# Two mixture-of-experts stages of a graph network kernel: scatter of node rows replaced by an inverted gather, output biases' products moved behind the expert loop

## The reference, cut to what matters

```python
# first layer: three-layer experts, gates are the softmax of the two best scores
for e in range(8):
    h = gelu(x @ W1[e] + b1[e]);  h = gelu(h @ W2[e] + b2[e])
    out += comb[..., e:e+1] * (h @ W3[e] + b3[e])
# second layer: two-layer experts, gates are the two best of the softmax
for e in range(8):
    h = gelu(flat_x @ w1[e] + b1[e])
    out += (h @ w2[e] + b2[e]) * gates[:, e:e+1]
x = x + out          # x inside the experts is layernorm(x)
```

## Time and profile before

| | us |
|---|---|
| median of 3 runs (2336.26 to 2338.91) | 2336.54 |
| the profiled execution's own time | 2320.56 |
| its span, first to last instruction | 2318.8 |
| PE busy | 2096.3 (90%) |
| DVE busy | 1424.1 (61%) |
| ACT busy | 921.7 (40%) |
| POOL busy | 395.6 (17%) |

### The profile page before, as it was taken

One profiled execution on the slowest core, in us unless ns is written; L12 is line 12 of the kernel. 1 busy time (PEld: TensorE's weight loads), 2 busy tenths in 40 slices (PEclk: granted clock), 3 DMA queues, 4 the chain that ended last, 5 costly groups with the idle time before them and its releaser, 6 DMA issues. The chain is left out here.

```text
span 2318.8 us, 32237 instructions
## 1 busy us (share of the span) xinstructions
PE 2096.3 (90%) x12766; PEld 2018.4 (87%) x12766; DVE 1424.1 (61%) x2283; ACT 921.7 (40%) x1220; POOL 395.6 (17%) x216
## 2 busy tenths in 40 slices
PE   6998999999999999999869949788889968999995
PEld 6898999998999999999849949687889947999994
DVE  7654555565763233333459963358985777888885
ACT  2342255554441111111127723125622225777772
POOL 1674200000302444443010022210000020000001
PEclk9999999999999999999969979899999968999997
DMA  6222233333340111110159851110122047999985
GB/s 222 43 49 64 89 121 132 117 116 143 110 143 21 62 42 51 52 52 11 56 198 353 314 194 62 48 46 28 65 75 76 1 155 277 380 368 372 374 346 212
DMA packets 121791, 326.89 MB, mean 141 GB/s; under 512 B 14376, under 2 KB 83016, under 8 KB 106410
## 3 DMA queue, kind: packets, MB, share of 16 engines
q1 hardware_dynamic: 96906, 265.66, 31.9%
q10 hardware_dynamic: 18976, 43.31, 5.2%
q0 software_dynamic: 5760, 15.86, 2.2%
HBM read 278.22 MB, written 46.49 MB: 140 GB/s over the span
## 5 line engine op out<-in xcount | busy, mean ns | idle before, releaser
L666 PE MATMUL banks<-weight_hi,xt_hi 128*128 128x384 f32 (+2 forms) x2208 | 738.3, 334 | 46.2 <-DVE xt_lo L1442 14.3
L669 PE MATMUL banks<-weight_lo,xt_hi 128*128 128x384 f32 (+2 forms) x2208 | 722.8, 327 | 0.0
L670 PE MATMUL banks<-weight_hi,xt_lo 128*128 128x384 f32 (+2 forms) x2208 | 722.3, 327 | 0.0
L666 PEld LDWEIGHTS banks<-weight_hi,xt_hi 128*128 128x128 f32 x2208 | 422.9, 192 | 58.1 <-issue 29.2
L669 PEld LDWEIGHTS banks<-weight_lo,xt_hi 128*128 128x128 f32 x2208 | 422.9, 192 | 0.4 <-issue 0.2
L670 PEld LDWEIGHTS banks<-weight_hi,xt_lo 128*128 128x128 f32 x2208 | 422.1, 191 | 0.0
L1908 DVE TENSOR_TENSOR weight_lo<-weight_raw,weight_hi 128x2304 fp32r<-128x2304 f32 (+2 forms) x153 | 341.0, 2243 | 52.0 <-ACT weight_hi L1170 50.8
L1170 ACT ACTIVATE weight_hi<-weight_raw 128x2304 fp32r<-128x2304 f32 (+2 forms) x153 | 285.8, 1881 | 88.1 <-PE banks L666 56.5
L868 POOL TENSOR_TENSOR weight_hi<-weight_raw,columns 128x2304 fp32r<-128x2304 f32 x20 | 80.6, 4028 | 690.1 <-DMA weight_raw<-L_gnn_root_in 322.6
L1670 DVE TENSOR_TENSOR held_lo<-banks,held_hi 128x384 fp32r<-128x384 f32 x80 | 44.6, 558 | 213.0 <-ACT held_hi L1096 213.0
L2528 PE MATMUL banks<-held_hi,a_rel 128*128 128x384 f32 (+1 forms) x550 | 171.5, 340 | 2.8 <-ACT a_rel L1111 2.8
(11 more groups left out here) (404 smaller groups left out, 3490.2 us busy)
## 6 DMA issues: line engine op xcount, KB each, us to landing
weight_raw<-L_ffn_w_in SPq DMA_DIRECT2D x102, 1152.0 KB, 7.1
weight_raw<-L_gnn_W_in SPq DMA_DIRECT2D x32, 1152.0 KB, 5.5
weight_raw<-L_ffn_W_in SPq DMA_DIRECT2D x17, 1152.0 KB, 8.4
products<-bias_rows SPq DMA_DIRECT2D x80, 192.0 KB, 1.9
slot_in<-slot_rows ACTq DMA_DIRECT2D x34, 384.0 KB, 5.3
slot_out<-bias_rows ACTq DMA_DIRECT2D x34, 384.0 KB, 6.5
weight_raw<-L_ffn_W_in SPq DMA_DIRECT2D x17, 576.0 KB, 8.0
product_back<-products SPq DMA_DIRECT2D x10, 960.0 KB, 4.7
```

What stands on the lines that cost most here:

```text
L666: ins = pe.matmul(dst, s[0], m[0], start=start, stop=False)
L669: pe.matmul(dst, s[0], m[1], start=False, stop=False)
L670: return pe.matmul(dst, s[1], m[0], start=False, stop=stop)
```

## The change

Routing. Instead of sending rows to their places, the kernel stores `XE` once to DRAM (`node_rows`, with a row 0 of zeros, then the nodes), by five plain DMAs that SP issues behind the first weight loads, and inverts the places on chip. DVE splits each place into slot and row, writes two one-hot arrays (`is_row` 10 x 128 wide, `in_slot` 10 x 18 wide, the latter multiplied by the node's number), and PE sums the ten products of them: bank 3 then holds for each slot and row the number of its node, or 0. DVE copies this to `slot_node`, and POOL gathers slot by slot from `node_rows` straight into `slot_in`, two slots at once and then one whenever PE has transposed the slot two before. The scatter, the ACT loads of slots and the clearing of 17 x 128 rows are gone. The arrays lie in tiles that are free at that time (`weight3_lo`, `bias_rows`, `more_of`, `through`, `top_at`), which is why DVE splits 2 instead of 4 units before the loop of stage 1.

Biases. The ten products and their additions move behind the loop over the slots, on PE and on DVE, and `out_b` is loaded late into a slot buffer. `slot_hot` is made after `slot_node` instead of right after the places.

```diff
-                pool.wait_ge(placed, 2 * (n + 1))
-                for t in range(TILES):
-                    for k in range(CHOSEN):
-                        j = t * CHOSEN + k
-                        pool.indirect_dma_start(out=slot_rows_dram, out_offset=bass.IndirectOffsetOnAxis(ap=place[:, j:j + 1], axis=0),
-                                                in_=XE[:, t, :], in_offset=None).then_inc(sent, 16)
+                pool.wait_ge(nodes_out, 16 * TILES * (n + 1))
+                pool.wait_ge(placed, 3 * (n + 1))
+                for v in range(XSLOTS):
+                    if v >= 2:
+                        pool.wait_ge(t_full[n], slot_groups(n, v - 2))
+                    pool.indirect_dma_start(out=slot_in[v % 2][:, :], out_offset=None, in_=node_rows_dram,
+                                            in_offset=bass.IndirectOffsetOnAxis(ap=slot_node[:, v:v + 1], axis=0)).then_inc(slot_ready[n][v % 2], 16)
...
+                    if prior >= 0 and not rows_sent:
+                        for t in range(TILES):
+                            sp.wait_ge(rows_ready, ROWS_FFN[n] + t + 1)
+                            sp.dma_start(node_rows_dram[1 + t * P:1 + (t + 1) * P, :], XE[:, t, :]).then_inc(nodes_out, 16)
+                        rows_sent = True
...
-            act.dma_start(slot_rows_dram.rearrange("(s p) d -> p s d", p=P), zero_row[:, :].unsqueeze(1).broadcast_to([P, XSLOTS, DIM])).then_inc(cleared, 16)
+            act.dma_start(node_rows_dram[0:1, :], zero_row[0:1, :]).then_inc(cleared, 16)
...
+                order.step(vec.tensor_scalar(slot_i, place[:, :], SLOT_ROWS.bit_length() - 1, None, ALU.arith_shift_right))
+                order.step(vec.tensor_copy(slot_f, slot_i))
+                order.step(vec.scalar_tensor_tensor(row_f, slot_f, -float(SLOT_ROWS), place_f[:, :], ALU.mult, ALU.add))
+                order.step(vec.tensor_tensor(in_slot, ..., ALU.is_equal))
+                order.step(vec.tensor_tensor(is_row, ..., ALU.is_equal))
+                vec.tensor_tensor(in_tiles, f32(in_tiles), node_id.unsqueeze(2).broadcast_to(of_tile), ALU.mult).then_inc(chosen_ready, 1)
...
+                vec.wait_ge(inverse_full, n + 1)
+                vec.tensor_copy(slot_node, ps[:, INVERSE_BANK, 0:XSLOTS]).then_inc(placed, 1)
...
-                add_products(PR_FFN[n], X)
+                # behind output(XSLOTS - 1): the same ten additions, then vec.wait_ge(prod_used, ...)
...
+                for j in range(CHOICES):
+                    ins = pe.matmul(ps[:, INVERSE_BANK, 0:EVEN_SLOTS], is_row[:, j, :], in_slot[:, j, :], start=j == 0, stop=j == CHOICES - 1)
...
                 pe.drain().then_inc(e_used[n], 1)
+                pe.wait_ge(gate_in, 16 * 3 * (n + 1))
+                for j in range(SET):
+                    ...
+                    pe.matmul(ps[:, (PR_FFN[n] + j) % 8, 0:WCOL], combT[:, t * P:(t + 1) * P], out_b[:, wcols(c)], start=True, stop=True).then_inc(prod_full, 1)
```

98 lines of the change are left out of this document (64 added, 34 removed).

## The result

| | before | changed |
|---|---|---|
| median, us | 2336.53 (2334.76 to 2342.97, 6 runs) | 2310.82 (2301.38 to 2318.50, 6 runs) |
| profiled execution, us | 2320.56 | 2301.38 |
| its span, us | 2318.8 | 2299.3 |

Ratio of the times 0.9889, 95% interval 0.9870 to 0.9909. Two further sets gave 0.9892 (0.9872 to 0.9911) and 0.9891 (0.9872 to 0.9910). The forecast was 2310.0 us, the time 2310.8. Its inside is not as good as its sum: stage 0 won 6 us instead of 10.5, stage 1 won 19 instead of 16.2.

A forecast was written before the change was run, and what follows sets the result against it. PE, without idle time in both loops, was taken as the bound, so the wait before each first product counted: -10.5 (stage 0) -16.2 (stage 1) +0.2 (end) = -26.5 us, from 2336.54 to 2310.0 us; range 2305 to 2322.

The forecast's parts named there:

- Steps 1 to 6: Both stages, inversion, gather, landing and transposes between places and first layer product: 14.4 us, where 24.97 and 30.68 stood.
- Both must end, so removing one alone would bring little: Ahead of both loops, bias products with additions and POOL's ten scatters run side by side; the change removes both.
- With four they would take 5 us back: Stage 1, four low parts ahead of the first product would end 18.3 us after the places; two end at 13.3.
- What follows the first product, cost 0: Inside both loops, what the change adds was to hide behind PE and cost nothing.
- fifteen gathers per stage, cost nothing: Inside the loops, a gather needs 13 us and fits into the 14.8 us between release and need in stage 0.
- transposes of `slot_in` in the loops wait for DMA: Named sign that the prediction is wrong: inside the loops PE's transposes of gathered rows wait for their data.
- slow landings: Rival, 12%: first gathers land in 8.7 instead of 3.4 us, losing 5.3 us twice; 2320.6 us.
- Stage 1, -16.2: Gain from places to first product in stage 1, 30.68 less 14.4 us; ends 16.4 and 10.5.
- The products behind the loop: Bias products at both loop ends: about 10 us in stage 0; cost 0 in stage 0, 0.2 us in stage 1.
- DVE held up by POOL: Rival, 10%: gather issues keep DVE from starting, 0.42 us in each of 15 stage 0 turns, 6.3 us; 2316.3 us.
- Second loop fed by DMA: Rival, 10%: stage 1's weight loads can't catch up, PE runs dry later and 5 us go; 2315 us.
- gathers late in each turn: Rival, 6%: stage 0 gathers land too late every turn; at 22 us the loop loses 54 us; 2364 us.

The follow-up runs named there:

- prod_front: Changed kernel with the ten bias products back ahead of the first slot's transposes, `out_b` in its own buffer; 2339.63 us, 1.0021 of the kernel before.
- scatter_tail: Kernel before with its scatters and slot loads kept, but the bias products and additions moved behind the loop; 2341.06 us, 1.0064 of the kernel before.
- lo4: Changed kernel with four low parts instead of two ahead of the first slot's in stage 1; 2307.67 us, 0.9933 of the kernel before.
- loads_late: Changed kernel, but in stage 0 SP issues no loop weight load until the second slot's rows have landed; 2298.30 us, 0.9895 of the kernel before.
- mark_first: issues_first, but in stage 0 a POOL fill behind the second gather's issue raises DVE's semaphore, no wait in stage 1; 2294.38 us, 0.9881 of the kernel before.
- after_third: The changed kernel unaltered, timed and profiled a third time; 2298.80 us, 0.9891 of the kernel before.
- comb_first: Changed kernel with DVE's two copies out of PSUM ahead of `slot_hot` instead of behind it; 2319.47 us, 0.9931 of the kernel before.
- issues_first: comb_first plus a DVE wait on a POOL semaphore behind the second gather, `slot_hot` first for two slots only; 2300.97 us, 0.9908 of the kernel before.
- warm: Changed kernel plus 14 unread products of 384 columns on PE behind the transposes of `comb`; 2318.84 us, 0.9927 of the kernel before.
- issues_warm: issues_first plus the 14 unread products of warm; 2303.31 us, 0.9914 of the kernel before.

## Why the prediction was right, point by point

- **Steps 1 to 6, the way from the places to the first product: right to 0.1 us in sum, and nearly so by term (stage 0).** Six operations end at 1176.46, 2.66 us after the places (2.65); ten products 2.31 us (2.0); the copy 0.18 (0.25); `slot_hot` and the issue end at 1182.26, 3.2 us after the copy (3.3); landing 3.1 (3.4); transposes to product 2.80 (2.74). The rule for the issue, end of the DVE operation plus 0.9, did this.
- **"Both must end, so removing one alone would bring little": right**, and stronger than said. Prod_front and scatter_tail are both slower than before.
- **"With four they would take 5 us back": right**, lo4.
- **What follows the first product, cost 0: wrong in stage 0, 4.2 us.** The step that failed is "fifteen gathers per stage, cost nothing": I priced the gathers inside the loop by the steady turns, and for them it holds (windows above). The second gather is not one of them. I knew that an issue is held for as long as a DVE operation runs, and used it for the first issue and for one operation of 2.56 us. Three low parts in a row with no gap between them act as one of 3.47 us, so the second issue ended at 1186.40, 3 us after SP's first weight load (1183.45), and behind the loads a landing of 3 us became one of 7.4. It was the sign that I had named ("transposes of `slot_in` in the loops wait for DMA"), and the rival "slow landings" with its right reason at the wrong gather: the first landed in 3.1 us, the second did not. 1.8 us of the 4.2 are lost at the second slot, mostly by waiting. The other 2.4 are the clock: the first product at 2.4 GHz came 14.0 us after the first of all (14.6 and 13.6 in the other two profiles, not 11, as the first expectation has it) instead of 6.7. That the late rows kept it down is not shown: loads_late and prod_front have no wait there and 13.5 and 13.8 us, and the second profile of the kernel before, with nothing late, has 10.2. Mark_first has 6.4. What decides it stays open.
- **Stage 1, -16.2: at the first product right (16.3), in the end 18.9.** Its second gather is held longer still, 5.38 us, but is needed later. From the first product to the second slot's transposes it took 6.7 to 7.3 us, 8.5 before, since the clock rose 0.7 us after the first product (1.7 in after_third), 4.3 before. That was luck of the clock, not forecast.
- **The products behind the loop: durations right, cost too low.** They take 8.3 us in stage 0 and 10.8 in stage 1 (about 10 forecast), the first three additions 1.85 us together, the later ones 1.28 us apart, as forecast. But the end of stage 1 is 1.1 us longer instead of 0.2. There the sums start at 2282.91 and run nearly without a gap, and so hold the last three issues (1.54, 1.68, 1.68 us); before, two were held (1.45, 1.68), and the last two took 0.95. The last issue ends 0.7 us later after the last copy than before, and the last tile's sums start 1.1 us later. So the catching up that I had counted as free costs 0.7 us; the rest is landing. In stage 0 the first sum stands 14.9, 17.5 and 15.0 us behind the last copy in three profiles, 13.8 and 15.0 in two of the kernel before: 1.4 us more on the mean, of a size with the scatter, and part of the +2.3 in the ledger, whose rest lies in the mixer between the stages, in code that is the same; I have no cause for it.
- **DVE held up by POOL: false.** The three low parts beside a gather's issue took 3.47 us, 3.48 before. Nor is DVE held where the issue starts first: in scatter_tail the issue of 11.10 us starts at 1917.01 and the four low parts at 1917.32, and it is the issue that is held: the low parts take 9.94 us, 9.95 in the earlier trace rows. The Trainium skill, page "SBUF — State Buffer", section "SBUF: two separate sides", describes something near this in its box on software DMAs: while VectorE runs an operation in a two-port mode, GpSimd can't write descriptors, and the DMA only seems blocked. The operations here are subtractions and comparisons with two inputs in SBUF, not the copies that the box speaks of; the trace agrees in that the issues end 0.8 to 0.9 us after them.
- **Second loop fed by DMA, gathers late in each turn, no gain: none of them came.** Stage 1 from the first product to the last copy took 366.2, 366.2 and 363.6 us, 367.2 and 368.9 before.
- **The sum.** -26.5 us was put on the median, which gave 2310.0; the three ratios say -25.9, -25.2 and -25.3 us, with intervals of 4 to 5 us either way. The stretch that the change touches got 21.7 us shorter in the profiles. A difference of 3 to 4 us between the two is open: the intervals reach down to it, and the part ahead of the places scatters by more. The step from the profiled execution to the median failed too: I took the 16 us between them to stay, and they were 9.4 (2301.38 and 2310.82). The profiled execution got 19.2 us faster, 7 less than the sum. So it is partly luck that 2310.0 fits: by the traces the mechanism was worth 5 us less than I said.

## What to carry to other kernels

In this kernel an indirect DMA issued on POOL was held not by the one DVE operation beside it but by the whole gapless row of operations with two inputs in SBUF; look for the next gap, and count what enters the DMA queues until then. When two chains end at the same time, price the change that removes both, and don't expect a share from each half: what is freed can start other work (in scatter_tail low parts, then weight loads) that collides with what is left. And when a start-up is shortened, check the second and the third request, not only the first. Take two profiles before a difference of 2 us gets a cause: the clock alone moved a start and an end by that much in a kernel that was the same.

## What the runs showed of the hardware

- An indirect DMA's issue on POOL ends 0.8 to 0.9 us after the end of the gapless DVE row that it falls into: 3.84 us beside three low parts (the changed kernel), 5.38 beside two of 2.5, 6.18 beside `slot_hot` and three, 10.33 and 11.10 beside four. It does so too where it starts 0.3 us before the row (11.10 us, scatter_tail), and the DVE row isn't longer for it. DVE's copies out of PSUM did not hold it (1.02 us in comb_first).
- A semaphore that POOL's queue raises behind such an issue is up before the issue has run (issues_first: by 0.5 us or more). One raised by a fill on its datapath is not (mark_first).
- The same gather lands 2.9 us after its issue with no weight loads issued ahead of it (loads_late) and 7.4 with weight loads ahead of it (changed kernel).
- With the same extra products, TensorE's clock fell back to 1.2 GHz at the fourth of the first slot's products in warm (idle 2.45 us ahead of the transposes, 1.24 ahead of the products) and stayed at 2.4 through all 18 in issues_warm (idle 1.20 and 1.24), where it was down after 3.83 us of idling.
- The first expert product at 2.4 GHz in stage 0 came 3.5 us (lo4, where the clock then fell once more) to 15.3 us (issues_first) after the first one over the profiles without the extra products, 6.7 and 10.2 us in the two profiles of the kernel before.
